# Moving the last attribute gathers of a graph network into ten other stages

## What is computed

```python
edge_index = jnp.stack([src, dst])
x = _layernorm(x + _L0_gnn_ref(x, edge_index, ...))          # two convolutions, 128 -> 64 -> 128
x = _layernorm(x + _L1_gnn_ref(x, edge_index, ...))          # mean of the neighbours, one dense layer
x = _layernorm(x + _L2_gnn_ref(x, edge_attr_128, src, dst, ...))
x = _layernorm(x + _L3_gnn_ref(x, edge_weight, ...))         # two attention convolutions
```

```python
h = x @ enc_W + enc_b
for l in range(num_layer):                                    # 5
    m = jax.nn.relu(h[src] + edge_attr)                       # edge_attr: 100000 x 128, float32
    agg = jax.ops.segment_sum(m, dst, num_segments=n)
    ...
```

## Time and profile before

| | |
|---|---|
| median of three runs | 9178.5 us (9175.4 to 9179.1) |
| profiled execution, its own time | 9176.6 us |
| its span | 9174.8 us |
| TensorE, VectorE, ScalarE, GpSimd busy | 73%, 61%, 53%, 63% |
| mean granted TensorE clock | 0.85 of full speed |

### The profile page before, as it was taken

The page is one execution under the profiler, slowest core; times in us unless marked ns, Lnnn a source line. Parts: engine busy times, 40 slices in busy tenths (PEclk is TensorE's granted clock), DMA queues, the critical chain, the costliest instruction groups (busy, mean ns, idle before and its releaser), DMA issues. The chain is left out here.

```text
span 9174.8 us, 256266 instructions
## 1 busy us (share of the span) xinstructions
PE 6695.5 (73%) x61749; PEld 5700.8 (62%) x61755; DVE 5579.0 (61%) x14982; ACT 4878.7 (53%) x13233; POOL 5804.0 (63%) x5857
## 2 busy tenths in 40 slices
PE   5547676878980798798898798798556665566664
PEld 1545555657970797797797797797445554455554
DVE  6865555555550666666666666666556667466667
ACT  3013334435440665665665665665566674466664
POOL 0566557757757774774774774774577774677773
PEclk8558888988995899899899899899777888778787
DMA  1235553435533775785784784774466673566663
GB/s 40 62 110 160 157 155 101 120 80 168 146 81 108 229 240 142 234 241 143 232 241 138 233 241 140 235 241 141 148 181 192 190 204 98 153 189 190 190 197 98
DMA packets 1221610, 1511.32 MB, mean 165 GB/s; under 512 B 206525, under 2 KB 806113, under 8 KB 1205014
## 3 DMA queue, kind: packets, MB, share of 16 engines
q1 hardware_dynamic: 1013494, 1055.75, 37.0%
q0 software_dynamic: 207712, 450.99, 19.9%
HBM read 1276.37 MB, written 229.67 MB: 164 GB/s over the span
## 5 line engine op out<-in xcount | busy, mean ns | idle before, releaser
L1988 POOL DMA_INDIRECT rings<-rows_key,pick x2682 | 2616.9, 976 | 1321.2 <-issue 746.2
L1245 POOL DMA_INDIRECT bigDEF<-rows_key_value,idx x1664 | 1646.9, 990 | 690.2 <-issue 656.8
L2117 PE MATMUL wide<-bigDEF,bigC 128*128 128x128 bf16 (+2 forms) x32256 | 1832.1, 215 | 340.6 <-DVE bigC L2203 148.3
L2117 PEld LDWEIGHTS wide<-bigDEF,bigC 128*128 128x128 bf16 x32256 | 1681.5, 100 | 508.8 <-issue 454.0
L2228 DVE TENSOR_TENSOR bigDEF<-bigDEF,part 128x128 f32 (+1 forms) x3576 | 1014.3, 284 | 996.5 <-PE part L2082 385.9
L2082 PE MATMUL part<-rings 128*128 128x128 f32 (+1 forms) x7152 | 1098.8, 293 | 564.6 <-ACT rings L2016 419.5
L2082 PEld LDWEIGHTS part<-rings 128*128 128x128 f32 (+1 forms) x7152 | 938.5, 187 | 635.9 <-issue 573.9
L2001 ACT COPY pick<-pairs 128x3 int32 (+1 forms) x1192 | 222.0, 189 | 1935.9 <-PE part L2082 1660.0
L2008 ACT ACTIVATE rings<-iota,pairs 128x128 f32<-128x128 f32 x3576 | 1173.2, 391 | 27.1 <-PE part L2082 21.8
L1988 POOL DMA_INDIRECT rings<-rows_hidden,pick x894 | 863.9, 966 | 457.9 <-issue 241.1
L2139 PE MATMUL lump<-bigDEF,bigC 128*128 128x256 f32 x3840 | 936.8, 388 | 20.5 <-DVE bigDEF L2189 20.3
(11 more groups left out here) (425 smaller groups left out, 10233.1 us busy)
## 6 DMA issues: line engine op xcount, KB each, us to landing
bigC<-sheaf_hots SPq DMA_DIRECT2D x1152, 256.0 KB
rings<-in_attr SPq DMA_DIRECT2D x2235, 64.0 KB
bigC<-sheaf_attr SPq DMA_DIRECT2D x120, 1024.0 KB
walk_value<-bigDEF SPq DMA_DIRECT2D x416, 256.0 KB
rings<-walk_value SPq DMA_DIRECT2D x416, 256.0 KB
rings<-sheaf_steps SPq DMA_DIRECT2D x192, 256.0 KB
sheaf_hots<-bigC SPq DMA_DIRECT2D x192, 256.0 KB
bigB<-sheaf_hots SPq DMA_DIRECT2D x192, 256.0 KB
```

The lines of the kernel that those rows point to most:

```text
L1245: e.indirect_dma_start(gbuf[:, g, r, :], None, table, bass.IndirectOffsetOnAxis(ap=c.idx[:, g, r:r + 1], axis=0)).then_inc(c.gathered[g].s ...
L1988: e.indirect_dma_start(gbuf[:, draw(n), r, 0:width], None, table, bass.IndirectOffsetOnAxis(ap=c.pick[:, draw(n), r:r + 1], axis=0)).then_ ...
L2117: last = e.matmul(to, hot, terms, start=x < LOT and x % batch == 0 and j == 2, stop=x >= MARCH - LOT, skip_group_check=True)
```

## The change

Two more units (4 in place of 2) are gathered in the second block of `_lots`, and its two iotas move to the head of the first block. The other 160 gathers go, in units of 4 tiles (FILL), into nine stages between table 1 and table 3: a `Fill` object holds the first tile, the number of units and the shelves (2, 3 or 4 of 512 columns, in places that the stage leaves free). In each stage `fill.fetch` stands last on GpSimd, and `fill.stow` last on SyncE, but in `_norm` ahead of the row stores. The counts are: table 1 2 units (8 gathers), mixed 1 7 (28), mixed 2 7 (28), dense 3 (12), norm 1 4 (16), mixed 3 7 (28), norm 2 6 (24), encoder dense 2 (8), table 3 2 (8). `_arrange` is gone. What is computed, and the number of gathers, stay the same; 40 stores of 256 KB and two of 512 KB stand where 22 of 512 KB stood.

```diff
--- before.py
+++ after.py
@@ -56,8 +56,9 @@
 UNIT = 8
 SHELVES = 4
+FILL = 4
 AHEAD = 24
-BESIDE = 2
+BESIDE = 4
...
         @block_.gpsimd
         def _(e):
+            e.iota(far_s, [[0, per], [P, steps]], base=P, channel_multiplier=0, allow_small_or_imprecise_dtypes=True
+                   ).then_inc(c.joined.sem, 1)
+            e.iota(lane, [[LOT, per], [0, steps]], base=0, channel_multiplier=0, allow_small_or_imprecise_dtypes=True
+                   ).then_inc(c.joined.sem, 1)
             for unit in range(AHEAD):
                 if unit % 2 == 0:
                     e.wait_ge(c.close.sem, c.close.at(unit // 2 + 1))
-                _fetch(c, e, unit, unit, shelves)
+                _fetch(c, e, 0, unit, shelves)
...
         @block_.gpsimd
         def _(e):
-            e.iota(far_s, [[0, per], [P, steps]], base=P, channel_multiplier=0, allow_small_or_imprecise_dtypes=True
-                   ).then_inc(c.joined.sem, 1)
-            e.iota(lane, [[LOT, per], [0, steps]], base=0, channel_multiplier=0, allow_small_or_imprecise_dtypes=True
-                   ).then_inc(c.joined.sem, 1)
             for k in range(BESIDE):
-                _fetch(c, e, AHEAD + k, k, shelves)
+                _fetch(c, e, AHEAD * UNIT, k, shelves)
...
-def _shelves(t, at):
-
-    return [t[:, at + k * UNIT * D:at + (k + 1) * UNIT * D].rearrange("p (a x) -> p a x", x=D) for k in range(SHELVES)]
-
-
-def _fetch(c, e, unit, k, shelves):
-
-    b = k % SHELVES
-    if k >= SHELVES:
-        e.wait_ge(c.stowed[b].sem, c.stowed[b].at(16 * (k // SHELVES)))
-    for a in range(UNIT):
-        at = unit * UNIT + a
+def _shelves(t, at, size, count):
+
+    return [t[:, at + k * size * D:at + (k + 1) * size * D].rearrange("p (a x) -> p a x", x=D) for k in range(count)]
+
+
+def _fetch(c, e, first, k, shelves):
+
+    b, use = k % len(shelves), k // len(shelves)
+    size = shelves[b].shape[1]
+    if use > 0:
+        e.wait_ge(c.stowed[b].sem, c.stowed[b].at(16 * use))
+    for a in range(size):
+        at = first + k * size + a
         e.indirect_dma_start(shelves[b][:, a, :], None, c.attr,
                              bass.IndirectOffsetOnAxis(ap=c.edgeS[:, at:at + 1], axis=0)).then_inc(c.fetched[b].sem, 16)
 
 
 def _stow(c, e, first, count, shelves):
 
-    per = LOT // UNIT
     for k in range(count):
-        b, unit = k % SHELVES, first + k
-        e.wait_ge(c.fetched[b].sem, c.fetched[b].at(16 * UNIT * (k // SHELVES + 1)))
-        e.dma_start(c.sorted_attr[unit // per, :, unit % per * UNIT:(unit % per + 1) * UNIT, :], shelves[b]
-                    ).then_inc(c.stowed[b].sem, 16)
-    for b in range(min(SHELVES, count)):
-        e.wait_ge(c.stowed[b].sem, c.stowed[b].at(16 * len(range(b, count, SHELVES))))
-
-
-def _stowed(c, count):
-
-    for b in range(SHELVES):
-        uses = len(range(b, count, SHELVES))
-        c.fetched[b].passed(16 * UNIT * uses)
+        b, use = k % len(shelves), k // len(shelves)
+        size = shelves[b].shape[1]
+        at = first + k * size
+        e.wait_ge(c.fetched[b].sem, c.fetched[b].at(16 * size * (use + 1)))
+        e.dma_start(c.sorted_attr[at // LOT, :, at % LOT:at % LOT + size, :], shelves[b]).then_inc(c.stowed[b].sem, 16)
+    for b in range(min(len(shelves), count)):
+        e.wait_ge(c.stowed[b].sem, c.stowed[b].at(16 * len(range(b, count, len(shelves)))))
+
+
+def _stowed(c, count, shelves):
+
+    for b, shelf in enumerate(shelves):
+        uses = len(range(b, count, len(shelves)))
+        c.fetched[b].passed(16 * shelf.shape[1] * uses)
         c.stowed[b].passed(16 * uses)
 
 
-def _arrange(c, first, shelves):
-
-    count = QUEUE // UNIT - first
-    with c.nc.Block() as block:
-        @block.gpsimd
-        def _(e):
-            for k in range(count):
-                _fetch(c, e, first + k, k, shelves)
-
-        @block.sync
-        def _(e):
-            _stow(c, e, first, count, shelves)
-    _stowed(c, count)
+class Fill:
+    def __init__(self, c, count, shelves):
+        self.c, self.count, self.shelves = c, count, shelves
+        self.first = c.filled
+        c.filled += count * FILL
+
+    def fetch(self, e):
+        for k in range(self.count):
+            _fetch(self.c, e, self.first, k, self.shelves)
+
+    def stow(self, e):
+        _stow(self.c, e, self.first, self.count, self.shelves)
+
+    def done(self):
+        _stowed(self.c, self.count, self.shelves)
...
@@ -1812,7 +1817,7 @@
-def _mixed(c, kind, table, agg, width, dram, room, begin=None, attr=None, weights=(), fresh=False):
+def _mixed(c, kind, table, agg, width, dram, room, begin=None, attr=None, weights=(), fresh=False, fill=None):
...
             if fresh:
                 for g in c.hotload:
                     e.wait_ge(g.sem, g.at(16 * SHEAVES * LEGS // HELD))
+            if fill:
+                fill.stow(e)
             if weights:
                 e.wait_ge(c.loaded.sem, c.loaded.at(0))
...
             with _loop(e, 0, rounds) as i:
                 for n in range(BODY):
                     fetch(i, n)
+            if fill:
+                fill.fetch(e)
...
@@ -2359,6 +2370,15 @@
+        if fill:
+            @block.gpsimd
+            def _(e):
+                fill.fetch(e)
+
+            @block.sync
+            def _(e):
+                fill.stow(e)
...
@@ -2673,6 +2715,8 @@
             for n in range(0, STEPS, 1 if late else 2):
                 e.tensor_tensor(part(x, n), part(x, n), part(plus, n), ALU.add).then_inc(c.joined.sem, 1)
+            if fill:
+                fill.fetch(e)
...
-        if out is not None:
+        if fill or out is not None:
             @block.sync
             def _(e):
...
+                if fill:
+                    fill.stow(e)
+                if out is not None:
+                    keep(e)
...
+        c.filled = (AHEAD + BESIDE) * UNIT
         room = _room(c, C, HID)
-        _table(c, B, hid, HID, other=F, op=ALU.mult, base=E_)
-        _mixed(c, "sum", hid, D_, HID, dram, room, begin=B, fresh=True)
+
+        def fill(count, t, at, shelves):
+            return Fill(c, count, _shelves(t, at, FILL, shelves))
+        _table(c, B, hid, HID, other=F, op=ALU.mult, base=E_, fill=fill(2, c.rings, 2560, 4))
+        _mixed(c, "sum", hid, D_, HID, dram, room, begin=B, fresh=True, fill=fill(7, room.spare, 0, 3))
         _table(c, B, hid, HID, other=F, op=ALU.mult, source=(D_, column["L0_gnn_b1"][h, :]))
-        _mixed(c, "sum", hid, D_, HID, dram, room, begin=B)
+        _mixed(c, "sum", hid, D_, HID, dram, room, begin=B, fill=fill(7, c.rings, 1152, 4))
         _dense(c, [([(c.W2g[:, :], D_)], B, column["L0_gnn_b2"], ACT.Identity, P)],
-               feed=(D_[h, :], D_[h, :], F[h, :], ALU.mult))
-        _norm(c, A, B, D_, out=keys)
+               feed=(D_[h, :], D_[h, :], F[h, :], ALU.mult), fill=fill(3, c.rings, 0, 4))
+        _norm(c, A, B, D_, out=keys, fill=fill(4, c.rings, 2560, 3))
 
 
         room = _room(c, B, D)
         _mixed(c, "sum", keys, D_, D, dram, room,
-               weights=[(C, dram.share.rearrange("(a x) -> a x", a=1).to_broadcast([P, COLS]))])
+               weights=[(C, dram.share.rearrange("(a x) -> a x", a=1).to_broadcast([P, COLS]))],
+               fill=fill(7, c.rings, DRAWS * BUNCH * P, 3))
         _dense(c, [([(c.W1T[:, :], D_)], B, column["L1_gnn_b"], ACT.Relu, P)],
                fore=(D_, D_, C, ALU.mult), feed=(D_, D_, A, ALU.add))
-        _norm(c, A, B, D_)
-
-
-        _dense(c, [([(c.encW[:, :], A)], B, column["L2_gnn_enc_b"], ACT.Identity, P)])
-        _table(c, B, keys)
+        _norm(c, A, B, D_, fill=fill(6, c.rings, 2560, 3))
+
+
+        _dense(c, [([(c.encW[:, :], A)], B, column["L2_gnn_enc_b"], ACT.Identity, P)], fill=fill(2, C, 0, 4))
+        _table(c, B, keys, fill=fill(2, C, 0, 4))
+        assert c.filled == QUEUE
         wide = (E_, F)
         room = _room(c, C, D)
-        _arrange(c, AHEAD + BESIDE, _shelves(C, 0))
```

More of the change, by code:

```diff
@@ L838, in _lots @@
     c.attr, c.sorted_attr = attr, sorted_attr
-    shelves = _shelves(C, 2048)
+    shelves = _shelves(C, 2048, UNIT, 4)
+    steps = n - 1
+    per = P // LOT
+    far_s, lane = (D[:, 5184 + i * 512:5184 + i * 512 + per * steps] for i in range(2))
     def lots(t, i):
@@ L1037, in _ @@
             e.wait_ge(c.moved.sem, c.moved.at(16))
-    _stowed(c, BESIDE)
+    _stowed(c, BESIDE, shelves)
     c.moved.passed(16)
@@ L1806, in _room @@
         r.stage = [left[:, k * size:(k + 1) * size] for k in range(4)]
+    r.spare = left
     tile, at = BUNCH * P, DRAWS * BUNCH * P
@@ L2282, in _ @@
             sum_up(final, 1, LOOSE * BUNCH)
+    if fill:
+        fill.done()
     for gate in (c.product, c.select, c.index):
@@ L2641, in _table, with _norm @@
         c.joined.passed(STEPS)
-def _norm(c, x, plus, rows, out=None, back=True, late=None):
+def _norm(c, x, plus, rows, out=None, back=True, late=None, fill=None):
     nc = c.nc
@@ L2661, in shelf, with keep @@
         return c.normal[:, at:at + P]
+    def keep(e):
```

(9 more changed lines are left out.)

26 lines of the change are left out of this document (9 added, 17 removed).

## The result

The changed kernel takes **9034.3 us** (median of four runs, 9023.3 to 9044.5) against 9178.8 of the kernel before in the same session: ratio 0.984, 95% interval 0.983 to 0.986. Forecast were 9037.5 us and a range of 9010 to 9075. The profiled execution has a span of 9039.5 us and took 9041.3 us.

The account below looks back on a forecast made before the run. The separate gather stage was taken to hold the whole chip for 226.3 us; removing it, less +85.3 us for gathers placed elsewhere, gave -141 us and 9037.5 us, with a range of 9010 to 9075.

Parts of the forecast that it names:

- The stage that goes: The separate gather stage before the first edge stage disappears, with nothing after it taking its time: -226.3 us.
- The three mixed stages: Gathers behind the last draws of mixed 1, 2 and 3 outlast the cover there: +14, +16.3 and +13.0 us.
- The 1 us put down for gathers beside the step loads: In mixed 1, gathers run beside the last step-list loads, for which VectorE waits: 1 us added.
- The end of 6.8 us: After a large stage's last gather come its landing, one last store and the barrier: 6.8 us.
- The short stages: Tables, norms and dense stages: SyncE's program is short and its barrier comes quicker, so the tail is 4.9 us.
- Dense of norm 1 and encoder dense: Their 12 and 8 gathers, with the tail, slightly outlast the stages: +0.5 and +1.5 us.
- Norm 1: Sixteen gathers and their stores put the row stores on SyncE 10 us late, 1 us of it regained: +9 us.
- Norm 2: 24 gathers after GpSimd's adds, plus 2 us for VectorE's work and the tail, lengthen it: +6.9 us.
- The tables: Tables 1 and 3: two fill stores stand behind all row stores and their landing, one more store time: +2.7 us each.
- Second block of `_lots`: Sixteen more gathers cost 20.0 us, less 1.25 for two iotas moved ahead at no cost: +18.7 us.
- The lock: VectorE holding the port pair shared with GpSimd blocks descriptor writes; taken for every gather, the net would be +184 us.
- the rival with 3.33 us each: Every new gather on the path is blocked like the first draw: 325 us more, 9363 us, slower than before; chance 2%.

Follow-up runs that it names:

- the seven shelves: Changed kernel with a shelf for each of mixed 1's seven units, so no gather there waits for a store; 9023.1 us.
- the spread kernel: Changed kernel with 30 of the 44 units one at a time between mixed 1's draws and 14 behind the draws elsewhere; 8956.3 us, ratio 0.977.
- the later places: The kernel with gathers between mixed 1's draws, but none among its first 31 bunches, one unit more in norm 2 and one in encoder dense; 8941.4 us, ratio 0.976.
- the stage of its own: Changed kernel with the 84 gathers of mixed 1, 2 and 3 put back into a separate stage before the edge layers; 9096.5 us.
- the repeat: The changed kernel run once more with no edit; 9034.6 us, ratio 0.985.

## Why the prediction was right

**The stage that goes: right.** 226.3 us, and nothing behind it took their place.

**The three mixed stages: right by the steps named, and in part by luck.** +13.2, +16.1, +13.4 against 14, 16.3 and 13.0. The last draws of mixed 2 lay 570.7 us into the stage before and 569.7 after, then 28 x 1.247 and the end. In mixed 1 the pause was forecast at 1367 to 1379.8, 13 us, and measured at 12.71; the seven shelves took it away and 11.6 us of the time. The 1 us put down for gathers beside the step loads can't be told from the spread: TensorE ended 40.0 and 40.3 us after the last draw without gathers, and 39.9 to 44.6 in the eight profiles with them; in the changed kernel it was done 10.8 us before the stage ended, so none of that is in its length. The luck is in mixed 2: the cover of 25.5 us in its rows was 21.0 to 22.0 in four other profiles, and the table compares with the same profile that the forecast was read from.

**The end of 6.8 us: right in size, wrong in its reason.** The forecast made it out of landing, store and SyncE's barrier, "since SyncE leaves the same kind of long program there". Without the last stores it was the same 6.8 us, and behind three multiplications it began again. The 2.3 us read as SyncE's barrier are SyncE waiting for GpSimd, whose DRAIN ended 6.5 to 6.6 us after its last instruction. The short stages do end sooner (4.0 and 4.15 us in the dense stage, 4.7 in norm 2), as forecast with 4.9; there GpSimd's DRAIN is over first, and what ends last is a landing or another engine.

**Dense of norm 1 and encoder dense: small terms, other cause.** The term of +0.5 came from 12 gathers and their end. They ended in time: the last one at 2085.38, with 4.0 us behind it 2089.4, and the stage began its successor only after the last matmuls, at 2092.4. It was +2.4 us, since its 32 matmuls took 21.70 us at 0.50 and not 19.27 at 0.59. In the encoder dense too the matmuls were over last (ScalarE, which takes their results, at 2827.9, SyncE at 2827.4): 13.33 us at 0.83 for 12.48 at 0.89. The working costed no clock. In the changed kernel TensorE had rested for 20 us, since the gathers ended mixed 2. In the kernel with twelve gathers there the dense stage took 20.4 us:

```profile
2008.00:2022.50 14.50, 9.75 (x44) 5.47 (x42) 7.54 (x24) 0.00 (x0) 6.56 (x7) 1.00 0.29 90
2022.70:2043.00 20.30, 11.72 (x32) 5.42 (x32) 7.78 (x16) 9.49 (x16) 12.46 (x12) 0.84 0.25 78
```

That is the spread kernel: 32 matmuls in 11.72 us instead of 21.70, and the gathers end the stage. But the kernel with the later places has the same work ahead and ran it at the slow clock:

```profile
1999.00:2014.50 15.50, 9.99 (x45) 5.63 (x43) 7.66 (x25) 0.00 (x0) 8.07 (x8) 1.00 0.27 89
2014.70:2038.20 23.50, 21.69 (x32) 10.37 (x32) 7.85 (x17) 9.50 (x16) 12.48 (x13) 0.51 0.22 67
```

Of the five profiles in which TensorE worked until the dense stage, three ran it slowly (before 19.27 us, the stage of its own 21.34 at 0.53, later places 21.69) and two fast (11.72, and 11.73 with 28 gathers there). In the seven in which it had rested for about 20 us the stage took 23.5 us each time. So a rested TensorE went with the slow clock each time, but rest alone does not explain it. By the Trainium skill (TensorE: Matmul & The Clock Gate, "Part 1: The HAM clock gate") the engine has two rates, 1.2 and 2.4 GHz, and goes to the low one when idle. The trace agrees: over the rest at the end of mixed 2 (2048.5 to 2068.9) the mean granted clock was 0.55. That a stage with matmuls one behind the other stays at the low one for 21.7 us after 15.5 us at the high one is measured here, and no run shows why.

**Norm 1: right step, too large a size.** +6.1 (+6.7 in the repeat) for 9. The row stores were forecast to start 10 us late and started 7 us late, since the sixteen gathers took 1.27 us each, start to start, and not 1.39. The stores of the fill were over 3.7 us behind the last gather and not 4.5. The row stores also ran 1 us faster, as allowed for. **Norm 2**: +5.6 for 6.9; two microseconds had been added there for VectorE's work, and the gathers needed 0.9 of them. **The tables**: +3.1 and +3.0 for 2.7, with the two stores last, as forecast.

**Second block of `_lots`: two small misses.** The iotas "ahead of the first half's gathers" were costed at nothing; the last gather of that block ends 1.1 us later than before, and the next block begins its own at 585.25. In the block itself I had taken 1.25 us off for them, and the stage grew by 19.9 us, the whole of 16 x 1.247. No run tested it; both lie inside 2 us.

**The lock: the trace took the row's side.** By the Trainium skill (SBUF — State Buffer, "SBUF: two separate sides") GpSimd can't write a gather's descriptors while a VectorE instruction holds the port pair that the two share. In the tails of the changed kernel the median gather took 0.944 us, and beside the sixteen 64x400 multiplications of the dense stage the first five took 1.15 to 1.26. Single gathers in the tails of the twelve profiles took up to 1.89 us. The forecast kept 1.25 to 1.39 start to start; the rival with 3.33 us each did not come.

The errors of the terms, from -2.9 (norm 1) to +1.9 (dense), cancel to half a microsecond. With a cover that differs by 4 us and last draws that differ by 5 and more from profile to profile, that closeness is partly luck; a forecast of this kind is good to 10 us or so.

## What to carry to other kernels

When work moves behind the last instruction of an engine, compute the new end of the stage as a chain of its own (last draw, gathers, end of block), since that chain repeated to 1 us in mixed 2 and 3 (to 3 us in mixed 1, where a store stands in it); what it replaces varied by 5 us, and should be read from more than one profile. Before filling the tails, look for waits inside the stage: 96 gathers between draws cost 3 us where the draws had slack, and pushed everything back where they had none. And look at which queue has to free the buffers: four more shelves were worth 12 us only because SyncE was late.

## What the runs showed that was not expected

- GpSimd's last instruction in mixed 2 with 28 gathers is followed by 6.8 us to the next stage and 7.4 us to its own next instruction, whether it is a gather or a multiplication, behind a loop or written-out code, with or without stores on SyncE; 6.5 us of it is GpSimd's DRAIN. In the dense stage the DRAIN ends after 2.0 to 2.7 us, and the stage, where the gathers end it, after 4.0 to 4.2.
- The same 32 matmuls of a dense stage took 11.7, 19.3 or 21.7 us in different profiles, at granted clocks of 0.84, 0.59 and 0.50 over the stage; two of the slow ones (21.3 and 21.7 us) came right after a stretch at 1.00.
- Unchanged stages of some 6180 us vary by 18 us between profiles, more than most terms of this forecast.
